# A routed mixture-of-experts stage: VectorE reads one packed plan word for each tile, SyncE stores the next tile's quarters ahead of loading this one's

## The reference

```
x = x + tanh(g_xattn) * mamba(ctx, z = layernorm(x))     # in_proj, conv of 4 taps, silu, scan of 16 states over 512 steps
h = layernorm(x)
scores  = softmax(h @ gate_w.T)                          # 16 experts
topk_w, topk_ids = top_k(scores, 6); topk_w /= sum(topk_w)
for each expert e:   out += combine[:, e] * (silu(h @ w13_e[:352].T) * (h @ w13_e[352:].T)) @ w2_e.T
out += (the same with the shared weights sw13, sw2, whose inner width is 704)
x = x + tanh(g_ffn) * out
```

## Time and profile before

| | us |
|---|---|
| median of 3 runs | 1445.77 (1439.89 to 1447.3) |
| the profiled execution | 1442.46 |
| its span, first to last instruction | 1440.7 |
| TensorE busy in it | 1321.2 (92%) |
| VectorE busy | 853.9 (59%) |
| ScalarE busy | 731.9 (51%) |
| GpSimd busy | 948.1 (66%) |

### The profile page before, as it was taken

The page is one execution under the profiler, slowest core; times in us unless marked ns, Lnnn a source line. Parts: engine busy times, 40 slices in busy tenths (PEclk is TensorE's granted clock), DMA queues, the critical chain, the costliest instruction groups (busy, mean ns, idle before and its releaser), DMA issues.

```text
span 1440.7 us, 31551 instructions
## 1 busy us (share of the span) xinstructions
PE 1321.2 (92%) x8064; PEld 1172.1 (81%) x8065; DVE 853.9 (59%) x1469; ACT 731.9 (51%) x1317; POOL 948.1 (66%) x671
## 2 busy tenths in 40 slices
PE   7897998998898899999889999999999999999995
PEld 3686887888888799999778878888888888788885
DVE  6878898888999854653344444444444444444442
ACT  5898897898889363333223333333332333333321
POOL 0588899998898657886446645566636665646632
PEclk8899999997999999999999999999999999999998
DMA  4121113221252554564677777888787777877862
GB/s 137 41 72 30 56 64 109 62 99 56 75 166 68 144 123 91 144 151 71 178 174 207 199 212 173 202 208 211 198 182 194 218 195 206 213 183 195 209 165 36
DMA packets 136276, 205.91 MB, mean 143 GB/s; under 512 B 20496, under 2 KB 74384, under 8 KB 134016
## 3 DMA queue, kind: packets, MB, share of 16 engines
q0 software_dynamic: 31024, 62.10, 23.7%
q1 hardware_dynamic: 101744, 102.33, 23.6%
q10 hardware_dynamic: 3440, 40.63, 7.8%
HBM read 130.99 MB, written 76.25 MB: 144 GB/s over the span
## 4 chain that ended last, share of the span: by engine, by line
PE 36%; DMA 14%; issue 7%; DVE 4%; DVEq 4%; POOL 3%; ACT 1%; POOLq 1%; ACTq 0%; SPq 0%
PE bank L1777 11%; PE bank L1757 10%; PE bank L1758 10%; DMA xs<-token_quarters 6%; DMA token_quarters<-xt 4%; DMA xt<-token_rows,gid 3%; PE bank L1768 2%; POOL w L1033 2%; DVEq L1435 2%; DVEq L1429 1%; DVE hs L1223 1%; PE bank L1667 1%; PE bank L1653 1%; ACT ah L908 1%; DVE xl L1423 1%
## 5 line engine op out<-in xcount | busy, mean ns | idle before, releaser
L1757 PE MATMUL bank<-w,xh 128*128 (+1 forms) x1088 | 370.3, 341 | 27.5 <-DVE am L1453 14.7
L995 POOL TENSOR_TENSOR hc<-hs,crow 128x512 f32<-128x512 f32 x254 | 322.0, 1299 | 89.0 <-DVE hs L1223 83.4
L1061 POOL DMA_INDIRECT out_x<-ys,aid x104 | 170.4, 1638 | 277.0 <-issue 234.3
L1758 PE MATMUL bank<-w,xh 128*128 (+1 forms) x1088 | 351.5, 324 | 0.0
L1223 DVE TENSOR_TENSOR_SCAN hs<-dA,bank 128x512 f32<-128x512 f32 x256 | 295.8, 1208 | 50.3 <-PE bank L1667 32.4
L1777 PE MATMUL bank<-w,ah 128*128 (+1 forms) x816 | 262.6, 403 | 20.3 <-DVE al L1459 19.8
L1757 PEld LDWEIGHTS bank<-w,xh 128*128 128x128 f32 x1088 | 204.9, 188 | 60.6 <-issue 56.8
L914 ACT COPY ys<-bank 128x512 f32<-128x512 f32 x136 | 79.8, 586 | 259.6 <-PE bank L1777 259.6
L1758 PEld LDWEIGHTS bank<-w,xh 128*128 128x128 f32 x1088 | 206.9, 190 | 2.3
L1777 PEld LDWEIGHTS bank<-w,ah 128*128 128x128 f32 x816 | 150.5, 190 | 52.5 <-issue 27.2
L1758 PE MATMUL bank<-w,xl 128*128 (+1 forms) x544 | 175.9, 323 | 0.0
(11 more groups left out here) (184 smaller groups left out, 1996.8 us busy)
## 6 DMA issues: line engine op xcount, KB each, us to landing
raws<-in_wall ACTq DMA_DIRECT2D x16, 2176.0 KB, 9.0
token_quarters<-xt SPq DMA_DIRECT2D x104, 256.0 KB, 4.3
xs<-token_quarters SPq DMA_DIRECT2D x104, 256.0 KB, 3.7
crow<-c_rows SPq DMA_DIRECT2D x64, 256.0 KB, 3.2
xt<-token_rows_turned SPq DMA_DIRECT2D x32, 256.0 KB, 3.1
out_x<-ys POOLq DMA_DIRECT2D x32, 256.0 KB, 4.1
token_rows<-rowb SPq DMA_DIRECT2D x4, 1028.0 KB, 6.1
xrow<-in_x SPq DMA_DIRECT2D x4, 1024.0 KB, 8.0
```

The source lines that it names most:

```text
L995: nc.gpsimd.tensor_tensor(hc[:, j, :], hs[:, j, :], crow[:, n % 4, :], ALU.mult).then_inc(hc_done, 1)
L1061: pool.indirect_dma_start(out_rows, bass.IndirectOffsetOnAxis(ap=aid[:, s:s + 1], axis=0), ys[:, s, :], None, bounds_check=TOKENS - 1, oob ...
L1757: nc.tensor.matmul(gate_bank[:, 0:I], xx, columns(w, off + ww + k * 2 * I, I), start=first, stop=last)
L1758: mm = nc.tensor.matmul(up_bank[:, 0:I], xx, columns(w, off + ww + k * 2 * I + I, I), start=first, stop=last)
```

## The change

Three pieces.

1. VectorE packs three values of the plan in one word for each tile (`packed`, `meta[:, 1]`, which nothing read before): next_weights' expert of tile t, the expert number of tile t + 1, and the list column of tile t + 5. `plan_of`(t) reads it at the head of tile t and takes it apart with remainders and divisions in registers. `take_weight`, `gather_ids` and `next_weights` get their values from it.
2. `add_ids` copies from `gid`, which still holds the tile's row numbers, instead of from `lists`. For that it moves: in tile t it is done for tile t + 1, ahead of `gather_ids`(t + 5), which overwrites the same slot of `gid`. Its wait is now for the scatter of tile t - 3, and two waits on VectorE's own copies are added.
3. SyncE's `move` is split. `put_quarters`(t + 1) is issued ahead of `set_quarters`(t). Each keeps its waits: `put_quarters`(t + 1) for gather(t + 1), `set_quarters`(t) for the store of tile t.

```diff
+                dve.wait_ge(meta_ready, 2)
+                n = NT - AHEAD
+                chained(nc.vector.scalar_tensor_tensor(out=packed[:, 0:n], in0=meta[:, 0, 1:n + 1], scalar=float(NX), in1=meta[:, 2, 0:n],
+                                                       op0=ALU.mult, op1=ALU.add))
+                chained(nc.vector.scalar_tensor_tensor(out=meta[:, 1, 0:n], in0=meta[:, 4, AHEAD:NT], scalar=float(NX * (NX + 1)),
+                                                       in1=packed[:, 0:n], op0=ALU.mult, op1=ALU.add))
...
-            def move(t, s, m):
+            def put_quarters(t, s, m=None):
 
                 rows_in(sp, t, s, m, "sp")
+                apart(sp, xt_turned, t - 3, "sp")
                 sp.dma_start(quarters_d[s].rearrange("a p j -> p a j"), xt[:, s, 0:H].rearrange("p (a j) -> p a j", a=G)).then_inc(put[s], 16)
+
+            def set_quarters(t, s, m=None):
+
                 of_slot(sp, put[s], t, m, "sp")
                 apart(sp, xt_turned, t - 3, "sp")
                 sp.dma_start(xs[:, s, :], quarters_d[s].rearrange("a (r g) j -> (a r) (g j)", g=G)).then_inc(moved[s], 16)
...
-            groups = routed_groups(sp)
-            with sp.Fori(0, groups) as i:
+            looped = sp.value_load(fours[0:1, 2:3], min_val=E // 4 - 2, max_val=ROUTED // 4 - 2)
+            put_quarters(NS, 0)
+            with sp.Fori(0, looped + 1) as i:
                 for k in range(4):
-                    move(4 * i + NS + k, k, i)
+                    put_quarters(4 * i + NS + k + 1, (k + 1) % 4, i + (k + 1) // 4)
+                    set_quarters(4 * i + NS + k, k, i)
...
-            def take_weight(t, s4, m=None):
-
-                if isinstance(t, int) and t < NS:
-                    return
-                e = dve.value_load(meta[0:1, 0, bass.ds(t, 1)], min_val=1, max_val=NX)
+            def plan_of(t):
+
+                word = dve.value_load(meta[0:1, 1, bass.ds(t, 1)], min_val=0, max_val=NX * (NX + 1) * NR - 1)
+                return dve.snap(word % NX), dve.snap(word // NX % (NX + 1)), dve.snap(word // (NX * (NX + 1)))
+
+            def take_weight(t, s4, number, m=None):
+
...
             def add_ids(t, s4):
 
+                apart(dve, gid_done, t + 1, "dve")
                 apart(dve, added[s4], through(t - 4, s4), "dve")
-                nc.vector.tensor_copy(aid[:, s4:s4 + 1], lists[:, bass.ds(ids_column(t), 1)]).then_inc(aid_done, 1)
+                nc.vector.tensor_copy(aid[:, s4:s4 + 1], gid[:, s4:s4 + 1]).then_inc(aid_done, 1)
...
+                split, number, column = plan_of(t)
+                turn(t + 1, after, m)
+                a_low(t - 1, 1 - s)
+                take_weight(t + 1, after, number, m)
+                add_ids(t + 1, after)
+                if gathers:
+                    apart(dve, aid_done, t + 2, "dve")
+                    gather_ids(t + AHEAD, after, column)
...
                 x_low(t + 1, 1 - s)
-                if adds:
-                    add_ids(t, s4)
                 multiply(t, s)
-
+                next_weights(t, split)
```

More of the change, by code:

```diff
@@ L391, in mamba_moe @@
         column = alloc(ctx, "column", [P, NT])
-        sloti = alloc(ctx, "sloti", [P, NT], I32)
-        odd = alloc(ctx, "odd", [P, NT], I32)
+        packed = alloc(ctx, "packed", [P, NT])
         fresh = alloc(ctx, "fresh", [P, NT])
@@ L396, in mamba_moe @@
         fours = alloc(ctx, "fours", [P, 3], I32)
-        second = alloc(ctx, "second", [P, WCOLS + 160])
+        second = alloc(ctx, "second", [P, WCOLS + 464])
         xs = alloc(ctx, "xs", [P, 4, TC * P])
@@ L695, in _ @@
             sp.wait_ge(meta_ready, 2)
-            groups = routed_groups(sp)
-            with sp.Fori(0, groups) as i:
+            looped = sp.value_load(fours[0:1, 2:3], min_val=E // 4 - 2, max_val=ROUTED // 4 - 2)
+            put_quarters(NS, 0)
+            with sp.Fori(0, looped + 1) as i:
                 for k in range(4):
-                    move(4 * i + NS + k, k, i)
+                    put_quarters(4 * i + NS + k + 1, (k + 1) % 4, i + (k + 1) // 4)
+                    set_quarters(4 * i + NS + k, k, i)
+            rest = tiles_but_12(sp) + 8
+            for k in range(3):
+                put_quarters(rest + k + 1, k + 1, looped + 1)
+                set_quarters(rest + k, k, looped + 1)
+            set_quarters(rest + 3, 3, looped + 1)
             tiles = tiles_but_12(sp) + 12
@@ L1398, in fill_table @@
                     chained(nc.vector.tensor_scalar(meta[:, 0, :], slot[:], 1.0, None, ALU.add))
-                    chained(nc.vector.tensor_copy(sloti[:], slot[:]))
-                    chained(nc.vector.tensor_scalar(odd[:], sloti[:], 1, None, ALU.bitwise_and))
-                    chained(nc.vector.tensor_scalar(meta[:, 1, :], odd[:], float(2 * WCOLS), None, ALU.mult))
                     return
@@ L1423, in x_low, with gather_ids @@
                 nc.vector.tensor_tensor(xl[:, s, :], source, xh[:, s, :], ALU.subtract).then_inc(xl_done, 1)
-            def take_weight(t, s4, m=None):
-                if isinstance(t, int) and t < NS:
-                    return
-                e = dve.value_load(meta[0:1, 0, bass.ds(t, 1)], min_val=1, max_val=NX)
+            def plan_of(t):
+                word = dve.value_load(meta[0:1, 1, bass.ds(t, 1)], min_val=0, max_val=NX * (NX + 1) * NR - 1)
+                return dve.snap(word % NX), dve.snap(word // NX % (NX + 1)), dve.snap(word // (NX * (NX + 1)))
+            def take_weight(t, s4, number, m=None):
                 rows_in(dve, t, s4, m, "dve")
                 at_least(dve, am_done, t - 1)
-                nc.vector.tensor_copy(cc[:, s4 % 2:s4 % 2 + 1], xt[:, s4, bass.ds(H - 1 + e, 1)]).then_inc(cc_done, 1)
+                nc.vector.tensor_copy(cc[:, s4 % 2:s4 % 2 + 1], xt[:, s4, bass.ds(H - 1 + number, 1)]).then_inc(cc_done, 1)
             def ids_column(t):
                 return dve.value_load(meta[0:1, 4, bass.ds(t, 1)], min_val=0, max_val=NR - 1)
-            def gather_ids(t, s4):
-                nc.vector.tensor_copy(gid[:, s4:s4 + 1], lists[:, bass.ds(ids_column(t), 1)]).then_inc(gid_done, 1)
+            def gather_ids(t, s4, column=None):
+                nc.vector.tensor_copy(gid[:, s4:s4 + 1], lists[:, bass.ds(ids_column(t) if column is None else column, 1)]).then_inc(gid_done, 1)
             def add_ids(t, s4):
+                apart(dve, gid_done, t + 1, "dve")
                 apart(dve, added[s4], through(t - 4, s4), "dve")
-                nc.vector.tensor_copy(aid[:, s4:s4 + 1], lists[:, bass.ds(ids_column(t), 1)]).then_inc(aid_done, 1)
+                nc.vector.tensor_copy(aid[:, s4:s4 + 1], gid[:, s4:s4 + 1]).then_inc(aid_done, 1)
             def multiply(t, s):
@@ L1469, in low_piece, with next_weights @@
                     low.then_inc(wl_done, 1)
-            def next_weights(t):
-                e = dve.value_load(meta[0:1, 2, bass.ds(t, 1)], min_val=0, max_val=NX - 1)
+            def next_weights(t, e):
                 with dve.If(e > 0):
@@ L1507, in beside, with tile @@
                         fill_table(i)
[L1509 to L1515, removed]
+            def tile(t, s4, gathers=False, m=None):
+                s, after = s4 % 2, (s4 + 1) % 4
+                if isinstance(t, int) and t < PEELED:
+                    a_low(t - 1, 1 - s)
                     beside(DVE_AFTER_A, t)
-                if isinstance(t, int) and t < NS:
                     for late in FIRST_ROWS.get(t, ()):
                         gather_ids(late, late % 4)
-                elif gathers:
-                    gather_ids(t + AHEAD, (s4 + 1) % 4)
+                    x_low(t + 1, 1 - s)
+                    multiply(t, s)
+                    return
+                split, number, column = plan_of(t)
+                turn(t + 1, after, m)
+                a_low(t - 1, 1 - s)
+                take_weight(t + 1, after, number, m)
[3 more added lines that the diff above has]
+                    gather_ids(t + AHEAD, after, column)
+                else:
+                    for late in FIRST_ROWS[t]:
+                        apart(dve, aid_done, t + 2, "dve")
+                        gather_ids(late, late % 4)
                 x_low(t + 1, 1 - s)
-                if adds:
-                    add_ids(t, s4)
                 multiply(t, s)
+                next_weights(t, split)
             dve.sem_inc(cc_done, NS)
@@ L1554, in _ @@
             tile(PEELED, PEELED % 4)
-            next_weights(PEELED)
             for k in range(1, 4):
-                tile(PEELED + k, (PEELED + k) % 4, True, True)
-                next_weights(PEELED + k)
+                tile(PEELED + k, (PEELED + k) % 4, True)
             with dve.Fori(0, groups - 1) as i:
                 for k in range(4):
-                    t = 4 * i + NS + 3 + k
-                    tile(t, (3 + k) % 4, True, True, i + 1)
-                    next_weights(t)
+                    tile(4 * i + NS + 3 + k, (3 + k) % 4, True, i + 1)
```

(1 more changed line is left out.)

## The result

The changed kernel takes 1476.5 us in the median (1476.35 to 1478.08, 4 runs), the kernel before 1446.47 beside it (1439.89 to 1447.3, 4 runs): a ratio of 1.022, with a 95% interval of 1.0189 to 1.0251. Slower, as forecast, and 11.5 us more than the 1465 of the forecast. The interval excludes no change; whether the loss is more than 2% it leaves open. Its profiled execution took 1478.08 us, 1476.3 of them its span.

The account below looks back on a forecast made before the run. TensorE, 92% busy, was taken to wait on VectorE's reads and late `xs` loads behind `split_low`. From 1442.5 us profiled, +22 in the stretch and -1 outside gave 1463.5; half the median's offset made 1465, range 1437 to 1480.

Parts of the forecast that it names:

- The reads: VectorE: four register reads per tile become one; `a_low` to `x_low` falls from 2.70 us, gaining at most about 11 us.
- The divisions: VectorE ahead of `turn`: about four divisions, 0.2 to 0.5 us, costed at nothing because they run under `multiply` and waits.
- The main term: An expert's first five tiles, from first tile t0: late load(t0+5) makes u(t0+5) - u(t0) 36.65 us, 31.5 without waits.
- the forecast's series: SyncE: load(t0+5) stands behind gather(t0+6), itself behind GpSimd's `split_low`; `turn`(82) starts at 1052.1 instead of 1049.25.
- Two of the signs that I named: `turn`(t0+5) waits 2 to 4 us at nearly each expert; u(t0) and u(t0+5) lie 36 to 37 us apart.
- the sum: Per expert 36.65 us plus 10.2 for later tiles, 46.85 against 45.25 now: +1.6, over 14 experts +22 us.
- `add_ids`' wait: VectorE in tile t0+3: waits for add(t0)'s scatter, 1 to 3 us once per expert, taken as covered by the later load.
- under the weight loads: Range only: `xs` load landings of 5.5 us under the weight loads; the sum took 4.4.
- (a): Rival: saved reads and shorter SyncE series win, if load(t0+5) costs nothing; -11 and -4, about 1430 us; chance 0.15.
- (b): Rival: gain and loss cancel with load landings of 2.5 to 3.3 us instead of 4.4; about 1445 us; chance 0.17.
- (c): Rival: `add_ids` in tile t0+3 waits for add(t0)'s scatter, +0.9 us per expert; about 1452 us; chance 0.08.

Follow-up runs that it names:

- small_load_after: The changed kernel with only the first eighth of each expert's raw weights loaded, from expert 4 on; 1472.61 us, ratio 1.0198.
- half_low_after: The changed kernel with GpSimd's `split_low` over half of the columns, the other half left stale; 1471.54 us, ratio 1.019.
- small_half_after: The changed kernel with both an eighth of the raw weights loaded and `split_low` over half of the columns; 1419.15 us, ratio 0.9822.
- vector_alone: The changed kernel with SyncE's loop of before (`move`), so VectorE's part alone; 1442.66 us, ratio 0.9979.
- old_add_vector: `vector_alone` with `add_ids` back behind `x_low`, reading `lists` itself and waiting for the scatter of tile t - 4; 1434.33 us, ratio 0.9945.
- share_vector: `vector_alone` with VectorE instead of GpSimd making the last quarter of the new weights' low part; 1427.15 us, ratio 0.9894.
- share_old_add: `old_add_vector` with VectorE making the last quarter of the new weights' low part; 1427.12 us, ratio 0.9891.

## Why the prediction was right, and where it fell short

*The reads.* Right in size: in place of the "issue" ahead of `gid` stand 26.6 us, 0.29 us for each tile, under the 30 that I named. From `a_low` to `x_low` I expected 1.6 to 1.7 us to be left; in tile 80 it is 1.33 (VectorE's timeline, after):

```profile
1061.78 0.56 DVE L1475 TENSOR_TENSOR al<-bank,ah 128x384 fp32r<-128x384 f32 x1 [2.73 <-ACT ah L918]
1062.25 0.14 DVE L1447 COPY cc<-xt 128x1 f32 x1
1062.56 0.15 DVE L1459 COPY aid<-gid 128x1 int32<-128x1 int32 x1 [0.16 <-issue]
1063.00 0.15 DVE L1453 COPY gid<-lists 128x1 int32 x1 [0.29 <-DVE aid L1459]
1063.11 0.69 DVE L1436 TENSOR_TENSOR xl<-bank,xh 128x512 fp32r<-128x512 f32 x1
```

The divisions were rightly costed at nothing: "issue" ahead of `turn` is 20.1 us in the stretch, where it was 27.8.

*The main term.* u(t0+5) - u(t0) was to be 36.65. For 77 it is 36.36 (TensorE's first matmuls of tiles 77 and 82, after):

```profile
1036.39 0.32 PE L1774 MATMUL bank<-w,xh 128*128 x1
...
1072.75 0.32 PE L1774 MATMUL bank<-w,xh 128*128 x1
```

In six of the 14 experts (77, 84, 97, 103, 109, 116) `turn`(t0+5) is followed by the next tile's matmuls after 3.5 to 3.6 us (forecast: 3.7): there the forecast's series decides. Five tiles take 36.80 us in the mean of the six, and store(t0+6) to u(t0+5) takes 8.96, where the forecast had 0.45 + 4.4 + 0.1 + 3.7 + 0.25 = 8.9. From u(t0) to store(t0+6) it had 27.75, measured 27.52 over all 14; for what follows 10.2, measured 10.31.

Two of the signs that I named came in part only. `turn`(t0+5) was to wait 2 to 4 us at nearly each expert: it waits 3.3 to 3.9 us in three, 4.4 to 5.8 in five, and at most 1.3 in the other six. And the five tiles lie between 36 and 37 us in three experts; they run from 35.77 to 40.41.

*The step that failed* is that the sum lets only load(t0+5) come late, and with it the ground on which I let tile t0+3 go: I looked there for `add_ids`' wait alone. load(t0+3) stands behind gather(t0+4), and so is issued behind the raw weights' load instead of ahead of it, in twelve of the 14. I had put the landings "under the weight loads" into the range (5.5 us), not into the sum, and that one is 9.9. In seven of the other eight experts (38, 45, 52, 58, 64, 70, 90) this load decides: `turn`(t0+3) waits 6.5 to 7.4 us for it, the next tile's matmuls follow `turn`(t0+5) only after 5.3 to 7.3 us, and the five tiles take 38.25 us. The eighth, 123, has no such wait, and tile t0+4 takes 10.98 us with the clock lowered. `small_load_after` and `half_low_after` show that the two loads are separate and that each is enough by itself.

So the forecast's mechanism is there, but decides in six experts of 14, and the right direction did not hang on it: `half_low_after`, in which `turn`(t0+5) hardly waits (0.48 us), is still at 1.019. That the time stayed in the range, 3.5 us below its upper end, with a second loss that the sum did not have, is in part luck: the two losses lie side by side (1.0198 with one, 1.019 with the other, 1.022 with both) where they could have added up.

*The clock* is the rest of it. Expert 70 is the worst, 40.41 us for five tiles. Windows of its tile 72, and two windows inside it:

```profile
997.37:1009.42 12.05, 8.33 (x37) 7.19 (x36) 3.29 (x8) 2.02 (x4) 9.27 (x3) 0.81 0.82 218
...
1000.50:1003.00 2.50, 1.20 (x8) 0.91 (x6) 0.00 (x0) 0.00 (x0) 2.50 (x1) 1.00 0.80 274
...
1007.00:1009.42 2.42, 2.42 (x7) 1.87 (x6) 0.73 (x1) 0.00 (x0) 0.11 (x1) 0.50 0.81 170
```

and TensorE's `down` in tile 72, and in tile 79, where it had waited less:

```profile
1005.42 1.22 PE L1794 MATMUL bank<-w,ah 128*128 x2 [3.72 <-DVE al L1475]
```

```profile
1056.60 0.72 PE L1794 MATMUL bank<-w,ah 128*128 x2 [1.66 <-DVE al L1475]
```

After the longer wait the granted clock is 0.50, which is the 1.2 GHz level, and the same two matmuls are shown with 1.22 us instead of 0.72. By the windows of the single tiles this happens in 11 of the 14 experts, in tile t0+2, or in t0+4 where that one waits (mean clock below 0.9). The waits of TensorE ahead of the fall are 2.1 to 3.7 us there; but one of 2.81 us, in tile 111, was followed by the full clock:

```profile
1289.42 0.72 PE L1794 MATMUL bank<-w,ah 128*128 x2 [2.81 <-DVE al L1475]
```

Over the stretch (1 - 0.97) x 671.5 = 20 us of TensorE's work at full speed are lost to it, part of it beside the series behind `split_low`. The Trainium skill, TensorE: Matmul & The Clock Gate, What's actually happening, lets the clock fall where TensorE stands idle; the trace agrees, with 3.72 us followed by 0.50 and 1.66 followed by 1.00. `small_half_after`, with its shorter waits, has 1.00 in its whole stretch. That the clock costs time is seen in the matmuls; how much of the loss it makes up by itself was not tried. It touches the forecast's own series too: in `small_load_after`, where the late load(t0+3) is gone, the five tiles still take 37.31 us, not 36.65, and from `turn`(t0+5) to the matmuls it takes 4.45 us in the mean, not 3.7; in eight of its experts tile t0+4 has a mean clock below 0.95.

*The sum.* 46.85 us per expert was forecast, 47.96 came: 14 x 1.11 = 15.5 us. Outside of the stretch -2.3 instead of -1, and 0.4 that I had rounded away (14 x 1.6 = 22.4, taken as 22). That makes the 14.6 by which the profiled execution, 1478.08, is above 1463.5. I had added 1.5 for the median, and the median came 1.6 below the profiled execution, so 11.5 are left.

*The rivals.* (a) fails on its condition: load(t0+5) does cost. VectorE's gain does exist, and is more than its 11 us, but only where nothing holds the series: 1443.7 to 1427.1, 16.6 us, once `split_low` is shorter; and behind the late loads 18 us. (b) needed landings of 2.5 to 3.3 us; `turn`(82) came 4.97 us after its load, and over the 14 experts it is 4.52 in the mean (3.3 to 5.7), where the forecast had 4.5. (c) is hidden in the changed kernel (9.4 us of waits ahead of `aid`), and comes out in `vector_alone` at the price that it was given: tile t0+3 takes 7.49 us instead of 6.59, +0.90 for each expert. Taking it away (`old_add_vector`) gave 8.3 us by the medians, of runs that were not taken together, and 5 by the ratios (0.9979 to 0.9945), not all of 12.6, since tile t0+5 rose from 6.91 to 7.51.

## What to carry to other kernels

When a queue's order is changed, write down for each moved issue which producer it now stands behind, and what other traffic starts in between: here the store of the next tile stood behind the one gather that comes after a 9.5 us operation, and a second load slipped, in expert 77, from 3.6 us ahead of a 2 MB transfer to 0.6 us behind it. Look at every place where the order shifts, not only at the one where the wait is longest; of two waits of the same length, side by side, removing one alone brought 4 to 5 us of the 57. Where two engines limit the same tiles (VectorE's reads and GpSimd's `split_low`), each improvement alone measured as no change (0.9979 and 0.9999), and together 1.1%: `share_vector` and `share_old_add`, both with 1427.1 us, are the fastest kernels here that leave nothing out.

## What the runs showed of the hardware

- A load of 256 KB, issued 0.6 us behind one of 2176 KB from another engine, took 9.9 us to its reader, where the median landing of its line in this kernel is 3.2 (2.6 to 11.6). In `half_low_after` 13 of the 14 loads of tile t0+3 took 9.5 to 10.9 us to their `turn`. The two in the changed kernel that were issued 0.35 us ahead of the large one took 5.0. The Trainium skill, DMA: Bandwidth & Descriptors, Issuing engines are not separate DMA queues, says that they interleave on the same engines; the trace agrees, and the price is about twice the 4.4 to 5.5 us that I had allowed.
- Behind one wait of 3.72 us on TensorE the granted clock was 0.50 for the rest of the tile, and in ten more experts it fell behind waits of 2.1 to 3.7 us; behind one of 1.66 and one of 2.81 us it did not. A late load can so cost more than its lateness.
- A copy on VectorE that waits for the VectorE copy just ahead of it costs 0.29 us, at each of 92 tiles.
